# A two-layer decoder on one core: another order of the slot attention's four engines, paced scatters with the weight in the row, and stage parameters from two queues

## The reference

```python
# gated slot attention, 16 heads of 128, 128 slots; per head and step:
gt = jnp.exp(g_t); bw = b_t[:, :, None] * w_t
Sk = Sk * gt[:, :, None, :] + k_t[..., :, None] * bw[:, :, None, :]
Sv = Sv * gt[..., None] + bw[..., None] * v_t[:, :, None, :]
s = jnp.einsum('bhd,bhdm->bhm', q_t, Sk) * SCALE
o_t = jnp.einsum('bhm,bhmd->bhd', jax.nn.softmax(s, axis=-1), Sv)
# q, k, v, w: silu of a causal convolution of 4 taps over h @ W; g = log_sigmoid(h @ Wf1 @ Wf2)
o = o * jax.lax.rsqrt(jnp.mean(o * o, axis=-1, keepdims=True) + EPS)
o = o * norm_w * jax.nn.sigmoid(gate)          # then o @ Wo
```

```python
top_w, top_i = jax.lax.top_k(probs, TOP_K)
combine = jnp.sum(jax.nn.one_hot(top_i, N_EXP) * top_w[..., None], axis=1)
y = jnp.einsum('eti,eih->eth', jax.nn.silu(g) * u, w_down_e)
routed = jnp.einsum('eth,te->th', y, combine)
x = x + (routed + sh).reshape(B, S, H)
```

## Time and profile before

| | before |
|---|---|
| median of 3 runs | 6733.94 us (6732.62 to 6741.56) |
| profiled execution | 6746.59 us, span 6744.8 us |
| PE busy | 5950.1 us, 88% |
| DVE / ACT / POOL busy | 65% / 58% / 28% |
| granted TensorE clock, mean | 0.950 |
| mean DMA | 31 GB/s |

### The profile page before, as it was taken

The page is one execution under the profiler, slowest core; times in us unless marked ns, Lnnn a source line. Parts: engine busy times, 40 slices in busy tenths (PEclk is TensorE's granted clock), DMA queues, the critical chain, the costliest instruction groups (busy, mean ns, idle before and its releaser), DMA issues. The chain is left out here.

```text
span 6744.8 us, 126497 instructions
## 1 busy us (share of the span) xinstructions
PE 5950.1 (88%) x45072; PEld 4612.7 (68%) x45072; DVE 4356.5 (65%) x9081; ACT 3899.1 (58%) x8601; POOL 1914.9 (28%) x2386
## 2 busy tenths in 40 slices
PE   8999999999999999999999999786886998978869
PEld 5777777777777777777777777676663665657646
DVE  4777777777777777777777777565772235766614
ACT  4766766766666677677666767553661323434313
POOL 2333333333333333333333333233113210001142
PEclk8999999999999999999999999887997999999989
DMA  6100000000000000000000000001002227010124
...
DMA packets 164244, 205.77 MB, mean 31 GB/s; under 512 B 22891, under 2 KB 149612, under 8 KB 162928
## 3 DMA queue, kind: packets, MB, share of 16 engines
...
## 5 line engine op out<-in xcount | busy, mean ns | idle before, releaser
L1532 ACT ACTIVATE gsa_gwva<-PSA,gsa_wcv 128x1024 f32<-128x1024 f32 x64 | 71.3, 1113 | 456.7 <-PE PSA L954 456.7
L1689 POOL TENSOR_TENSOR gsa_amb<-gsa_aab,gsa_yb 128x256 f32<-128x256 f32 x64 | 67.6, 1057 | 888.4 <-ACT gsa_aab L1549 888.4
L1711 POOL TENSOR_TENSOR gsa_ama<-gsa_aaa,gsa_ya 128x256 f32<-128x256 f32 x64 | 69.9, 1093 | 860.0 <-ACT gsa_aaa L1614 860.0
L1604 ACT ACTIVATE gsa_gwvb<-PSA,gsa_wcv 128x1024 f32<-128x1024 f32 x64 | 71.3, 1113 | 411.4 <-PE PSA L1112 411.4
L456 ACT ACTIVATE ffn0b_sl<-PSA 128x512 f32<-128x512 f32 x48 | 28.5, 597 | 265.4 <-PE PSA L162 181.0
L263 DVE TENSOR_TENSOR ffn0b_hidden<-ffn0b_sl,PSA 128x512 f32<-128x512 f32 x48 | 32.9, 686 | 204.7 <-ACT ffn0b_sl L456 177.1
L949 PE MATMUL PSA<-XT,gsa_wa 128*128 128x512 f32 x256 | 137.1, 662 | 29.6 <-issue 21.5
L1695 POOL TENSOR_TENSOR gsa_ssa<-gsa_ssa,gsa_neghalf 128x4 f32<-128x4 f32 x64 | 64.4, 1007 | 272.9 <-DVE gsa_ssa L1315 272.9
L1904 PE MATMUL PSA<-mlstm_XC,mlstm_WIF 128*128 128x128 f32 x512 | 94.5, 360 | 49.5 <-ACT mlstm_XC L2069 49.5
L2157 POOL TENSOR_TENSOR mlstm_rs<-mlstm_wide,mlstm_neghalf 128x16 f32<-128x16 f32 x32 | 95.4, 2983 | 142.7 <-DVE mlstm_wide L2034 142.7
L1716 POOL TENSOR_TENSOR gsa_ssb<-gsa_ssb,gsa_neghalf 128x4 f32<-128x4 f32 x64 | 64.4, 1007 | 246.1 <-DVE gsa_ssb L1439 246.1
...
## 6 DMA issues: line engine op xcount, KB each, us to landing
...
```

Of the source, the lines that this page charges most:

```text
L1532: nc.scalar.activation(GWVa[:, 512:1536].rearrange("p (k t) -> p k t", k=2), PSA[:, 0:0 + 2, :], ACT.Copy, scale=WCV[:, 11:12]).then_inc(c ...
L1604: nc.scalar.activation(GWVb[:, 512:1536].rearrange("p (k t) -> p k t", k=2), PSA[:, 4:4 + 2, :], ACT.Copy, scale=WCV[:, 11:12]).then_inc(c ...
L1711: nc.gpsimd.tensor_tensor(blocks(AMa[:, 0, :], 2), righttiles(AAa[:, :, 0:128], 2), rightblocks(Ya[:, 0, 0:512], 2), ALU.mult).then_inc(re ...
```

## The change

Three parts; what is computed stays the same.

```diff
-def moe(nc, io, X, PS, IDENT, shared, name, prefix, chunks, lead, gated, store=None):
+def moe(nc, io, X, PS, IDENT, shared, name, prefix, chunks, lead, gated, paced, store=None):
...
-                        for j in range(4):
-                            xs = X[:, g * 1024 + j * 256:g * 1024 + (j + 1) * 256]
-                            last = nc.vector.scalar_tensor_tensor(xs, zbank(g)[:, k, j, :], W12[:, k, 4 * g + j:4 * g + j + 1], xs, ALU.mult, ALU.add)
-                        last.then_inc(combined_by_dve, 1)
+                        xs = X[:, g * 1024:(g + 1) * 1024]
+                        nc.vector.tensor_tensor(xs, zbank(g)[:, k, :, :].rearrange("p i d -> p (i d)"), xs, ALU.add).then_inc(combined_by_dve, 1)
...
                 def weights():
+                    dve.wait_ge(marked, 16)
...
+                        nc.vector.tensor_copy(HK[:, :, 257], W12[:, 0, :]).then_inc(weights_by_dve, 1)
...
                     if step == 1:
+                        weights()
                         keep_counts()
...
-                    if step == 4:
-                        weights()
...
-                    nc.scalar.activation(Y[t % YS][:, :], PS[6 + t % 2][:, 0:256], ACT.Copy).then_inc(result_by_act, 1)
+                    nc.scalar.activation(Y[t % YS][:, :], PS[6 + t % 2][:, 0:256], ACT.Copy, scale=XS[t % ROWS][:, 257:258]).then_inc(result_by_act, 1)
...
                 def scatter(k, i, done):
+                    if paced:
+                        pool.wait_ge(hidden_by_dve, min(LEAD, 5 + (32 * k + i) // 2))
...
+                pool.wait_ge(weights_by_dve, 3 if gated else 5)
...
-                    pool.wait_ge(remarked_by_pool, half + 1)
+                    nc.gpsimd.tensor_copy(HK[:, 16 * half:16 * half + 16, 257], W12[:, 1, 16 * half:16 * half + 16]).then_inc(remarked_by_pool, 1)
+                    pool.wait_ge(remarked_by_pool, 2 * half + 2)
...
+                        sp.wait_ge(result_by_act, t - ROWS + 1)
...
-    moe(nc, io, X, PS, IDENT, shared, "ffn0b", "e0", 6, 4, True)
+    moe(nc, io, X, PS, IDENT, shared, "ffn0b", "e0", 6, 6, True, True)
...
-    moe(nc, io, X, PS, IDENT, shared, "ffn1b", "e1", 3, 5, False, store)
+    moe(nc, io, X, PS, IDENT, shared, "ffn1b", "e1", 3, 6, False, False, store)
```

**3. Starts.** Of the parameters of ffn0a, infini and cross four or five go out on ACT's queue. DVE does the first statistics before it waits; the first transposes of PE no longer wait for parameters. In ffn0a the weights that DVE folds come first, under a semaphore of their own:

```diff
+                statistics(0)
+                normalize(0)
+                dve.wait_ge(weighed, 64)
+                for W in (WQ, WK):
+                    for c in range(2):
                         last = nc.vector.tensor_scalar(W[:, c, :], W[:, c, :], LNW[:, c:c + 1], None, ALU.mult)
                 last.then_inc(folded_by_dve, 1)
...
+                nc.scalar.dma_start(PM[:, :], io["pair_mask"]).then_inc(loads, 16)
+                nc.scalar.dma_start(BC[:, :], io["f0_bcols"]).then_inc(loads, 16)
+                nc.scalar.dma_start(SIN[:, :], io["sin"]).then_inc(loads, 16)
+                nc.scalar.dma_start(COS[:, :], io["cos"]).then_inc(loads, 16)
+                nc.scalar.dma_start(NM[:, :], io["neg_causal_seq"]).then_inc(loads, 16)
```

675 lines of the change are left out of this document (357 added, 318 removed).

## The result

| | before | after |
|---|---|---|
| median | 6737.75 us (4 runs) | 6397.93 us (6390.95 to 6417.55, 4 runs) |
| ratio, 95% interval | | 0.950 (0.9477 to 0.9523) |
| profiled execution, span | 6744.8 us | 6396.9 us |
| granted clock, mean | 0.950 | 0.964 |

A forecast was written before the change was run, and what follows sets the result against it. PE, busy 88% of the span, bounds the kernel, so time is won where it idles or runs slow. −160 − 55 + 5 − 20 = −230 from 6746.6 gives 6516.6, or 6504 on the median's scale; range 6410 to 6610.

The forecast's parts named there:

- The slot attention term: Slot attention: reordering work on four engines removes PE's waits, 1.27 us in each of 128 halves, taken as −160 us.
- (2) and (3): Slot attention: output-gate sigmoid ahead of the SiLU, and two PE weight groups before the transposes; 1.04 us a half.
- The 0.23 at L1015: Slot attention: PE's wait before the second weights goes, as its DVE product no longer stands behind the convolutions; 0.23 us.
- I count 0: Slot attention: gain from a faster clock if waits cause the slow one; counted 0, up to −75 us.
- Rival (c): Slot attention gives more: gates' 0.53 wait and half the slow clock go too; −405 in all, 6329, halfway 6417; chance 0.13.
- Mixtures: First mixture of experts: paced scatters and a lead of 36 steps for 24 remove PE's 58.2 us stall; together −55.
- The +3 for a later start of the rows: First mixture: with the longer lead, rows begin later after the lead's end, partly hidden; +3 us.
- Rival (a): First mixture's lead: pacing cures nothing, the engines stand for another cause; total −172, 6562 us; chance 0.10.
- Second mixture: Second mixture: unpaced lead of 18 steps for 15 keeps the stall and delays the result loads; +5 us (0 to +15).
- a share over 0.72 in the last 50 us: Second mixture's end: sign that the DMA engines run fuller than the 0.72 share of before.
- Starts: Starts of ffn0a, infini and cross: reordered loads, a second queue, earlier statistics; −6.5, −5 and −9, sum −20 us.
- rival (d): Slot attention: the chain of decays becomes the loop's bound and the kernel gets slower, +71, 6805 us; chance 0.03.

The follow-up runs named there:

- e7: The kernel before with only ACT's output-gate sigmoid moved next to the decay gate's, PE's order untouched: 6744.12 us for 6643.21, ratio 1.0153.
- e4: The changed kernel with PE's two groups of weights put back behind the gwv transposes: 6956.88 us for 6643.21 of before, ratio 1.0472.
- e11: The changed kernel with only the second of PE's two weight groups (level 1) put back behind the transposes: 6573.18 us for 6646.35 of before, ratio 0.9886.
- e5: The changed kernel without pacing of the first mixture's scatters, lead still 36 steps: 6464.98 us.
- e13: The changed kernel run again without a new edit, on a chip that stalls: 6403.11 us for 6734.0 of before, ratio 0.9513.
- e8: The changed kernel with three scatters a step instead of two in the first mixture and a lead of 30 steps: 6407.47 us.
- e2: The kernel before with only the mixture-of-experts part of the change: 6629.78 us for 6643.21, ratio 0.998.

## Why the prediction was wrong

**The slot attention term.** "(2) and (3) win 1.04 a half. The 0.23 at L1015 goes too", and so 1.27 × 128 = 163, taken as −160, is the step that failed, by size: the stage gave 276. It priced a wait at its idle time alone and put the slow clock at nothing. The mechanism was right: the named waits shrank, the gates' wait stayed, the chain of decays did not get in the way. Measured from the starts of all halves in both traces:

- The usual half went from 32.13 to 30.17: −1.96, for −1.27. Listed idle gives 1.16 at the transposes (0.41 was left, not 0.53) and 0.23 at L1015. The rest is that a stop, a place where PE has to wait between two groups, costs more than its idle time. Where PE runs on, a group's last matmul overlaps the next group by 0.16; where it stops it does not. Before, a half had five such stops (one with a wait of 0.12 that no row of a wait shows), after three. Two stops less make 0.32, and that wait 0.12; 0.13 is left to small pitches. In all (1.96 − 1.27) × 128 = 88 of the 116.
- 28 of the 96 halves away from the loop's turns were 0.85 longer before, with the lower clock behind the wait of 1.6. After, none is. That is 24. The prediction saw the clock of 0.98, priced it at up to 75, and wrote "I count 0". e7, with the wait lengthened and PE's order untouched, shows that the wait brings it; e4 and e11 bring it back in after's order.
- At the ends of the stage (its first half and its last, unpaired part) 16 more; the turns of the loop cost 11 more than before, where their waits grew from 21.5 to 38.5. That growth was not foreseen, and no run says why.

That is 251 + 24 + 16 − 11 = 280, for 276. Up to 30 of it can be the chance named at the result, so what the prediction missed by its own terms is 86 to 116.

**The range.** Rival (c) had the right direction and partly the wrong place: it let the gates' 0.53 go, which stayed. The range's low end, 6410, was its halfway point (6417), and the result lies 12 below. What it says of the clock came true in part: the halves with a low stretch went. That this had to be so can't be said beforehand from before's trace: in e11 waits of 1.3, shorter than before's, cost more clock than before's 1.6.

**Mixtures.** −58.1 for −55: the step held on a chip that stalls, and e5 shows that pacing does it. The +3 for a later start of the rows was 0.4 (3.29 of idle for 2.87). Rival (a) falls. The Trainium skill's "A DMA cannot be slowed by a compute op, and vice versa" ("SBUF — State Buffer", section "SBUF: two separate sides") stands as it is worded: nothing here shows a slowed operand, yet scatters and a standing PE go together in e5 and e13, and e8 parts them by the pace alone. It is not a guide to whether such a stall exists. But the prediction took the stall for a property of the program alone, and the same program runs without it on other chips: in e2, where nothing stalls, the change's mixtures are worth 13, not 56. That the −55 came so near is luck in this: the result was taken on a chip that stalls.

**Second mixture.** +2.5 for +5 on a chip that stalls, −9.6 on one that does not. The result loads now start here:

```profile
6360.21 2.04 SPq L555 DMA_DIRECT2D ffn1b_WGU<-results  x4
```

From there to the end it takes 36.7 us at a DMA share of 0.98, for 47.5 at 0.78 before; the prediction had 37.4 with full engines. Its sign, a share over 0.72 in the last 50 us, was drawn too wide: windows of that length show 0.74 after and 0.75 before. The prediction overlooked the wait for the expert rows, since in the trace of before the stall had hidden it.

**Starts.** −15.5 for −20. infini and cross to a microsecond. At ffn0a the projection waits 4.22 for the router's weights, the last parameter on SP's queue. The prediction let a load land 2.2 after its issue and had all of them landed with the fold; here the four loads that the fold needs, issued by 4408.73, are there at 4412.97, and the router's, issued by 4410.16, at 4415.4, 4.2 and 5.2 later. The saving from the first DMA to the projection is 4.8, 4.3 and 8.2. By the Trainium skill ("DMA: Bandwidth & Descriptors", section "Issuing engines are not separate DMA queues") the second queue saves only time to issue, 6.6 by the pitch of 0.47; the 17.3 measured have 10.7 beyond that, which the order of the loads and the earlier statistics give. No run here parts those two.

**The slower rival (d)** never came near: ACT's idle late in the half grew, to 1.31 and 1.56 (at 1014.85 and 1017.50 in the half shown above).

## What stays open

Why 64 scatters at 1.27 us stop the engines in three of five jobs (the result's counted as one) and not in the other two was not settled. Pauses between the scatters are the lever: two or three a step don't stall, an unbroken row does, behind its 19th. What stands in the way between matmuls, which the profile calls "issue", no row tells. That fetches of instructions wait behind the scatters is a guess that the trace of e5 speaks against. Its DMA queues from 4840 to 4930, while PE stands and starts again nine times, are these two, and none of the kind "instruction":

```profile
q0 software_dynamic: 2465, 7.11, 21.3%
q1 hardware_dynamic: 864, 0.81, 3.2%
```

So PE went on at 4857.02 and at 4878.31 with no fetch of instructions in between that the trace shows. Nor is it shown why at a wait of the same 1.3 us the clock falls in one half and not in the next.
